# Recurrences with forget, input and candidate gates as three products, and attention's inputs in strips

## What is computed

```python
def rnn(x, h0, Wx, Wh, b):                       # layer 0
    h = tanh(x[t] @ Wx + b + h @ Wh)             # for t in 0..511
def lstm(x, h0, Wx, Wh, b):                      # layer 1
    a = x[t] @ Wx + b + h @ Wh                   # for t in 0..511
    i, f, o = sigmoid(a[:H]), sigmoid(a[H:2H]), sigmoid(a[2H:3H])
    g = tanh(a[3H:])
    c = f * c + i * g
    h = o * tanh(c)
x = x + rnn(x, cond, ...)
x = x + lstm(x, cond, ...)
x = x + transformer_block(x, cond, ...)          # layer 2: attention and feed-forward
x = x + mixture_of_experts(x, cond, ...)         # layer 3: two of four experts and a shared one
```

## Time and profile before

| | us |
|---|---|
| median of 3 runs | 2344.58 |
| lowest and highest | 2342.88, 2344.84 |
| the profiled execution | 2343.05 |
| its span | 2341.3 |
| recurrences: first and last write of `Hs` | 18.9, 1184.2 |
| PE, DVE, ACT, POOL busy | 2207.2, 1581.1, 1257.8, 560.5 |

### The profile page before, as it was taken

One profiled execution on the slowest core, in us unless ns is written; L12 is line 12 of the kernel. 1 busy time (PEld: TensorE's weight loads), 2 busy tenths in 40 slices (PEclk: granted clock), 3 DMA queues, 4 the chain that ended last, 5 costly groups with the idle time before them and its releaser, 6 DMA issues. The chain is left out here.

```text
span 2341.3 us, 94850 instructions
## 1 busy us (share of the span) xinstructions
PE 2207.2 (94%) x39004; PEld 1452.3 (62%) x39004; DVE 1581.1 (68%) x7316; ACT 1257.8 (54%) x4381; POOL 560.5 (24%) x1178
## 2 busy tenths in 40 slices
PE   8899999999999999999987699999999999999999
PEld 6677777777777777777743256464646556464666
DVE  5777777777777777777747684765747576674530
ACT  4555555555555555555565664647575564656432
POOL 0222222242221422214223031322213131221100
PEclk9999999999999999999998899999999999999999
DMA  4111111101000000000010200303030120302020
GB/s 119 36 38 31 38 40 42 37 25 32 29 31 27 22 27 29 31 27 18 23 69 1 88 35 1 131 1 131 1 131 1 38 94 1 131 1 104 0 86 9
DMA packets 51874, 102.64 MB, mean 44 GB/s; under 512 B 10468, under 2 KB 33380, under 8 KB 47348
## 3 DMA queue, kind: packets, MB, share of 16 engines
q1 hardware_dynamic: 48036, 94.06, 11.8%
q10 hardware_dynamic: 3408, 2.52, 0.4%
HBM read 75.53 MB, written 21.04 MB: 41 GB/s over the span
## 5 line engine op out<-in xcount | busy, mean ns | idle before, releaser
L135 PE MATMUL psFI<-wh,Hs 128*8 128x128 f32 (+3 forms) x8192 | 324.7, 276 | 61.0 <-DVE Hs L250 47.8
L135 PE MATMUL psOR<-wh,RH 128*16 128x128 f32 (+3 forms) x8320 | 321.5, 272 | 2.2 <-ACT RH L338 2.0
L135 PEld LDWEIGHTS psFI<-wh,Hs 128*8 128x8 f32 (+3 forms) x8192 | 182.2, 99 | 179.3 <-DVE Hs L250 179.3
L2054 ACT ACTIVATE pexp<-bank 128x1024 f32<-128x1024 f32 x256 | 244.3, 1023 | 36.1 <-PE bank L1384 35.9
L338 ACT ACTIVATE RH<-RT 128x16 f32<-128x16 f32 x512 | 110.9, 217 | 261.5 <-DVE RT L254 261.5
L1262 PE MATMUL bank<-x3T,ew 128*128 128x512 f32 x512 | 238.7, 593 | 0.0
L234 DVE STREAM_TRANSPOSE FIT<-psFI 128x128 f32<-128x128 f32 x512 | 162.0, 316 | 101.0 <-PE psFI L135 98.4
L329 ACT ACTIVATE sFI<-FIT 128x32 f32<-128x32 f32 x512 | 118.6, 232 | 200.4 <-DVE FIT L234 195.5
L135 PE MATMUL psG<-wh,Hs 128*8 128x64 f32 (+3 forms) x8192 | 208.6, 219 | 0.4 <-issue 0.4
L135 PEld LDWEIGHTS psOR<-wh,RH 128*16 128x16 f32 (+1 forms) x8320 | 205.7, 104 | 4.8 <-ACT RH L338 3.7
L1276 PE MATMUL bank<-ew,hidden 128*128 128x256 f32 x864 | 201.0, 379 | 0.0
(11 more groups left out here) (366 smaller groups left out, 4227.9 us busy)
## 6 DMA issues: line engine op xcount, KB each, us to landing
ew<-in_ew SPq DMA_DIRECT2D x32, 1024.0 KB, 9.1
qkv_scratch<-qkvr SPq DMA_DIRECT2D x31, 384.0 KB, 2.8
big<-qkv_scratch SPq DMA_DIRECT2D x7, 1536.0 KB, 7.8
XX<-in_xT SPq DMA_DIRECT2D x31, 256.0 KB, 2.7
x_scratch<-xr SPq DMA_DIRECT2D x32, 128.5 KB, 2.4
x<-x_scratch SPq DMA_DIRECT2D x8, 514.0 KB, 9.7
ada<-ada_scratch SPq DMA_DIRECT2D x8, 512.0 KB, 8.5
out_x<-x SPq DMA_DIRECT2D x7, 512.0 KB, 3.3
```

What stands on the lines that cost most here:

```text
L135: last = pe.matmul(bank[32 * j:32 * j + width, :], state(k), weights[:, k, j, cols], start=False, stop=k == KC - 1, tile_position=(0, 32 * ...
L2054: up(act.activation(M.pexp[:, n % 2, 2 * pr:2 * pr + 2, :], M.PS[pr][:, :, :], ACT.Exp, scale=1.0 / math.sqrt(HD)), "exps")
```

## The change

**Three products.** `psFI` becomes `psF` and `psI`, with 64 columns and two banks each. `FIT` becomes `FT` and `IT`. The loop makes the forget product, the input product and the candidate product, each with a raise of its semaphore (`FI` is raised twice a step). VectorE makes three transposes, ScalarE one sigmoid for forget and one for input. `gw` waits for forget's sigmoid only, the scan for input's too. The seeding bias copy and the inputs' product of the pair are split in the same way.

**Banks.** Both buffers of `psG` lie in one bank, and `psA` and `psB` share one. So TensorE waits at s = 2 for the next group's bias before it writes the candidate product, and for this slot's `GT` before it writes the inputs of the next group. The transposes of x2 wait until the outputs of q, k and v of the chunk two before have been taken (`qkv_out` instead of `zT_out`), also in `last_rows_back`.

**ScalarE's order.** The bias copies for s = 0, 1, 2, attention's copies and the heads' work stand ahead of the RNN's tanh (`tR`), not behind it; the bias copy at s = 3 stays behind.

**Strips.** Attention's 128 x 128 transposes and products in the loop go as four matmuls of 32 output partitions each, with a tile position for each (`strips`); the transposes become matmuls with the identity. VectorE still takes q, k and v out of `psB`.

```diff
@@ tensor, one slot
-                    products(R.psFI[g % 2], h, width, R.wh, F_I).then_inc(sem["FI"], 1)
+                    products(R.psF[g % 2], h, width, R.wh, F_).then_inc(sem["FI"], 1)
+                    products(R.psI[g % 2], h, width, R.wh, I_).then_inc(sem["FI"], 1)
+                    if s == 2 and g + 1 - FIRST < PIECES:
+                        pe.wait_ge(sem["bG"], g + 2 - FIRST)
                     products(R.psG[g % 2], h, width, R.wh, G_).then_inc(sem["G"], 1)
...
                 elif s == 1:
-                    inputs_of_group(g + 1, R.psFI, F_I, "bFI")
+                    inputs_of_group(g + 1, R.psF, F_, lambda q: (sem["bFI"], 2 * q + 1))
+                    inputs_of_group(g + 1, R.psI, I_, lambda q: (sem["bFI"], 2 * q + 2))
                 elif s == 2:
-                    inputs_of_group(g + 1, R.psG, G_, "bG", "X1")
+                    if lstm(i):
+                        pe.wait_ge(sem["gT"], n + 1)
+                    inputs_of_group(g + 1, R.psG, G_, lambda q: (sem["bG"], q + 1))
@@ vector, one slot
-                    dve.wait_ge(sem["FI"], n + 1)
-                    dve.transpose(flat(R.FIT), R.psFI[g % 2]).then_inc(sem["fiT"], 1)
+                    dve.wait_ge(sem["FI"], 2 * n + 1)
+                    dve.transpose(flat(R.FT), R.psF[g % 2]).then_inc(sem["fiT"], 1)
+                    dve.wait_ge(sem["FI"], 2 * n + 2)
+                    dve.transpose(flat(R.IT), R.psI[g % 2]).then_inc(sem["fiT"], 1)
                     dve.wait_ge(sem["G"], n + 1)
                     dve.transpose(flat(R.GT), R.psG[g % 2]).then_inc(sem["gT"], 1)
-                    dve.wait_ge(sem["sFI"], n + 1)
+                    dve.wait_ge(sem["sFI"], 2 * n + 1)
...
                     dve.wait_ge(sem["w"], n + 1)
+                    dve.wait_ge(sem["sFI"], 2 * n + 2)
                     dve.wait_ge(sem["tG"], n + 1)
@@ scalar, one slot
-                    act.activation(R.sFI[:, :, :, 1].rearrange("p g (k b) -> p (g k) b", k=KC), R.FIT[:, :, at_four:at_four + NB], ACT.Sigmoid).then_inc(sem["sFI"], 1)
+                    act.activation(by_block(second_scan(R.sFI[:, 0])), R.FT[:, :, at_four:at_four + NB], ACT.Sigmoid).then_inc(sem["sFI"], 1)
+                    act.wait_ge(sem["fiT"], 2 * n + 2)
+                    act.activation(by_block(second_scan(R.sFI[:, 1])), R.IT[:, :, at_four:at_four + NB], ACT.Sigmoid).then_inc(sem["sFI"], 1)
@@ attention's inputs
+        def strips(out, stationary, moving, start, stop):
+            for j in range(4):
+                at = slice(32 * j, 32 * j + 32)
+                last = pe.matmul(out[at], stationary[:, at], moving, start=start, stop=stop, tile_position=(0, 32 * j), skip_group_check=True)
+            return last
...
-                    last = pe.matmul(self.psB[:, half * P:(half + 1) * P], self.zT[:, k, :], self.wqkv[:, k, n * D + half * P:n * D + (half + 1) * P],
-                                     start=k == 0, stop=k == KC - 1, skip_group_check=True)
+                    last = strips(self.psB[:, half * P:(half + 1) * P], self.zT[:, k, :], self.wqkv[:, k, n * D + half * P:n * D + (half + 1) * P],
+                                  k == 0, k == KC - 1)
@@ last_rows_back
-        pe.wait_ge(*self.at("zT_out", c - 2))
+        pe.wait_ge(*self.at("qkv_out", c - 2))
```

More of the change, by code:

```diff
@@ L80 @@
     SLOTS = T + LAG
[L81 removed]
+    SIGNALS = ("FI", "G", "OR", "XX", "sFI", "tG", "sO", "tR", "tC", "bFI", "bG", "bOR", "fiT", "gT", "rT", "w", "c",
                "oT", "hL", "hR", "x1", "xx", "x2", "x_in_0", "x_in_1", "x_in_2", "ld_wx0", "ld_wh0", "ld_bias", "ld_states",
@@ L98, in __init__ @@
         self.zero = sb("zero", [P, P])
-        self.FIT, self.GT, self.RT = sb("FIT", [P, 2 * KC, 32]), sb("GT", [P, KC, 32]), sb("RT", [P, KC, 32])
+        self.FT, self.IT, self.GT, self.RT = (sb(n, [P, KC, 32]) for n in ("FT", "IT", "GT", "RT"))
         self.sFI, self.gw, self.cc = sb("sFI", [P, 2, KC * NB, 2]), sb("gw", [P, KC * NB, 2]), sb("cc", [P, KC * NB, 2])
@@ L102, in __init__ @@
         self.tC = sb("tC", [P, KC, NB])
-        self.psFI, self.psOR = ([ps(f"{n}{i}", 128) for i in range(2)] for n in ("psFI", "psOR"))
-        self.psG = [ps(f"psG{i}", 64) for i in range(2)]
+        self.psF, self.psI = ([ps(f"{n}{i}", 64) for i in range(2)] for n in ("psF", "psI"))
+        self.bothG = ps("psG", 128)
+        self.psG = [self.bothG[:, 64 * i:64 * i + 64] for i in range(2)]
+        self.psOR = [ps(f"psOR{i}", 128) for i in range(2)]
         self.sem = {n: ctx.enter_context(nc.semaphore(n)) for n in self.SIGNALS}
@@ L167, in inputs_of_group @@
                 x = piece_of(R.x1, q)
-                last = products(bank[g % 2], lambda k: x[:, k, :], 32, R.wx, cols)
-                if raises:
-                    last.then_inc(sem[raises], 1)
+                products(bank[g % 2], lambda k: x[:, k, :], 32, R.wx, cols)
             inputs_made = F.tensor_engine(pe, lambda c: R.x2[c % 2], sem["x2"])
             pe.wait_ge(sem["zeroed"], 1)
-            for bank in R.psOR + R.psFI + R.psG:
+            for bank in R.psOR + R.psF + R.psI + [R.bothG]:
                 last = pe.matmul(bank, R.zero[:, :], R.zero[:, 0:bank.shape[1]], start=True, stop=True)
@@ L344, in _ @@
                     bias_of_pair(2 * g + 2)
-                else:
+                inputs_made(i)
+                Q.scalar_slot(act, i)
+                if rnn(i):
+                    act.wait_ge(sem["rT"], i + 1)
+                    act.activation(r_of(i), R.RT[:, :, at_pair:at_pair + NB], ACT.Tanh).then_inc(sem["tR"], 1)
+                if s == 3:
                     if lstm(i):
@@ L756, in slot @@
                         if c == 0:
-                            pe.wait_ge(self.ada_made, 2)
+                            pe.wait_ge(self.ada_made, 3)
                         if c >= 2:
-                            pe.wait_ge(*self.at("zT_out", c - 2))
+                            pe.wait_ge(*self.at("qkv_out", c - 2))
                     columns = self.psA[:, 0:D].rearrange("p (j k u) -> p j k u", k=KC, u=32)[:, :, o, :]
-                    last = pe.transpose(columns, x2(c)[:, o, :], self.W.I[:, :])
+                    last = strips(columns, x2(c)[:, o, :], self.W.I[:, :], True, True)
                     if o == 1:
@@ L768, in slot @@
                         pe.wait_ge(*self.at("xT_out", c + 1))
-                    last = pe.transpose(self.psA[:, k * P:(k + 1) * P], self.z[:, k * P:(k + 1) * P], self.W.I[:, :])
+                    last = strips(self.psA[:, k * P:(k + 1) * P], self.z[:, k * P:(k + 1) * P], self.W.I[:, :], True, True)
                     if k == 1:
@@ L806, in vector_engine @@
         C = self.vector
-        m, d, k, small, e, s1 = (self.S[:, i:i + 1] for i in (1, 5, 6, 9, 10, 13))
+        m, d, k, small, e = (self.S[:, i:i + 1] for i in (1, 5, 6, 9, 10))
         def slot(i):
@@ L1117, in kept_busy @@
         for _ in range(n):
-            pe.matmul(self.F.psA[:, :], self.F.wqkv[:, 0, 0:P], self.F.wqkv[:, 1, 0:512], start=True, stop=True)
+            pe.matmul(self.F.ps[:, :], self.F.wqkv[:, 0, 0:P], self.F.wqkv[:, 1, 0:512], start=True, stop=True)
     def last_transposes(self, pe):
```

33 lines of the change are left out of this document (13 added, 20 removed).

## The result

The changed kernel takes **2605.07 us** (median of 4 runs, 2600.39 to 2606.4) against 2344.71 for the kernel before on the same chip: 1.111 times as long, interval 1.109 to 1.113. The forecast was 2319.

A forecast was written before the change was run, and what follows sets the result against it. The recurrence's chain, 2.28 us a step, was taken as the bound. Gains of 15.8, 8.3 and 2.0 (26.1 us) off 2343.05, plus 0.4 tail, gave 2317.4, adjusted to the runs' median: 2319; range 2313 to 2326 (0.62).

The forecast's parts named there:

- What bounds the kernel: Recurrence loop: one chain of 2.28 us a step bounds it, not TensorE, which idles 0.25 us awaiting `Hs`.
- The three thin products: Gate products at each step's start: at 0.23 us each, the candidate product starts only 0.01 us later.
- (a): Gate products: candidate product comes later than 0.01 us; at +0.03, 2329 to 2333 us; chance 0.13.
- (b): Gate products: thin products go at their weight loads' pace, 0.27 or 0.34 us; 10 or 82 us slower; chance 0.07.
- The transposes: VectorE's gate transposes: 64-column ones take 0.23 to 0.24 us; `GT` about 0.95 after the first product in light steps.
- Rival (c): VectorE's gate transposes do not overlap, 0.23 us each; 2346 us, no change; chance 0.07.
- Some 0.07 us to spare: Candidate branch before the scan: slack beside the forget/input branch, contributing to a gain of 0.06 us a step.
- The strips: Attention's 128-wide products: four strips should save most of the 0.21 us idle issue, off the path; priced zero.
- The rival I gave to TensorE as the bound: Attention strips: were TensorE the bound, 14 products in each of 31 chunks save 91 us, giving 2252; chance 0.01.
- ScalarE's order: Bias copies ahead of the RNN's tanh: they fit into ScalarE's 0.49 us of idle time; price zero.
- The tail: First transpose behind the loop waits for the last `qkvr` and starts 0.4 us later: +0.4 us.
- Rival (d): TensorE's clock: the lighter engine falls to 1.2 GHz, some 0.6 us a step; far above 2400; chance 0.02.

The follow-up runs named there:

- light_order_b: light_b with the scan's three waits reordered so the tanh's is written first and the multiply's last: 2349.74 us (1.0026 of the kernel before).
- before_act: The kernel before with only ScalarE's new order (bias copies, attention's copies, heads' work ahead of the RNN's tanh): 2343.12 us (0.9993).
- after_two: The changed kernel with the scan's wait for input's sigmoid moved to the multiply, leaving the scan two waits: 2614.83 us (1.115).
- pad13: The kernel before with 13 tiny matmuls of zeros and their loads added per step in steps 40 to 499: 2590.38 us (1.106).
- pad7: The kernel before with 7 tiny matmuls of zeros and their loads added per step: 2417.56 us (1.032).
- nostrips: The changed kernel with attention's transposes and products 128 wide again, one instruction in place of four: 2548.40 us (1.088).
- before_strips: The kernel before with only attention's transposes and products split into strips: 2348.01 us (1.0019).
- thin_light: The changed kernel without strips and without the inputs' products of forget, input and candidate gate in steps 40 to 500: 2494.42 us (1.064).
- light_b: The changed kernel without strips, every inputs' product of steps 40 to 499 cut to a single matmul: 2385.56 us (1.018).
- before_swap_b: The kernel before with the scan's two waits swapped, the tanh's ahead of the multiply's: 2377.47 us (1.0147).

## Where the prediction was right and where it failed

**What bounds the kernel.** Right for the kernel before: the chain of one step. Wrong as a statement about what can bound it. I read the busy time of TensorE and its clock and took "waits 0.25 us a step" for room. The room in instructions, 58.7 against some 66 per us, was 12%, and the change asked for 40% more. No step of the working counted them: their price was put at nothing without a reason, and this is the step that cost most, some 242 us. Counting what `products` and the strips write, 132 loads and matmuls a step against 184, would have been the first sign.

**The three thin products.** They start at 419.93, 420.17 and 420.39: the candidate product 0.46 behind the first, as forecast. Rivals (a) and (b), a slower pace of the products, did not come. What a thin product costs is not its place in the row but 32 more instructions a step, 16 loads and 16 matmuls, and the inputs' product of it.

**The transposes.** `FT` comes 0.49 behind the first product, `IT` 0.22 later, `GT` 0.22 after that, at 0.93 (forecast about 0.95, light steps). They take 0.25 rather than 0.23. Rival (c) is refuted: `IT` and `GT` start when their products allow.

**"Some 0.07 us to spare".** This is the step that failed in the critical path. The sum takes the scan to start 0.03 behind the tanh. With the tanh's wait last in a row of three it starts 0.13 behind, and 0.10 was already there in the earlier trace rows, which I read as slack of 0.07. From `GT` to the scan it is 0.63 in the step above, not 0.52 (and 0.59 before). Instead of -0.06 a step came out at +0.036: 511 x 0.036 = 18 us. light_order_b shows the -0.06 once the wait is placed so.

**The strips.** Their idle issue of 0.2 us did go; priced at zero, they cost 57 us in after (2605.07 - 2548.40) through 12 instructions a step. The rival I gave to TensorE as the bound looked at idle time per product, the wrong quantity, and it counts 14 such products a chunk where there are 16.

**ScalarE's order.** Price zero, right (before_act).

**The tail.** The first transpose behind the loop waits for the last `qkvr`, as said:

```profile
1445.71 0.48 DVE L871 SCALAR_TENSOR_TENSOR qkvr<-psAB,Sr,bqkv 128x256 f32<-128x256 f32 x1
...
1446.33 0.41 PE L588 MATMUL psAB<-I,x2c 128*128 128x128 f32 x2 [1.58 <-DVE qkvr L871]
```

1446.33 is 1.06 behind the last `Hs` (1445.27), against 0.58 in the earlier trace rows: +0.48, forecast +0.4.

**The clock.** Rival (d) did not come: 1.00 in the stretch above, 0.99 over the span.

**The account.** Of 260 us in the loop, 18 are the longer step; the other 242, by subtraction, are the supply of instructions. The direct count for 100 to 1100 us: 235 of 258 block boundaries with a gap of over 0.3 us, 210 us together. The 356 steps in it are longer than undisturbed ones by 356 x (2.805 - 2.305) = 178 us; the rest of the gaps, I take it, fell where TensorE would have waited for `Hs` anyway.

What sets 3.8 us for a block stays open. In after its parts are, as medians, 1.26 us from the start of a block to the start of the next packet, 1.10 for the packet and 1.39 from its landing to the next block. Packets were never closer than 3.3 us in any of these kernels. No run here changed anything but the number and spacing of instructions.

## What to carry to other kernels

Count the instructions of each engine per step beside its busy time: splitting a wide fp32 product into thin ones, or a 128-wide one into strips, multiplies their number and hardly shows in busy time, and TensorE got at most some 66 per us here. Idle "issue" at changing products, at equal distances in instructions, is its sign. A gap of 0.1 us between a releaser's end and an instruction with several waits is not slack before it has been compared with a hand-over by a single wait; the semaphore that comes last belongs into the wait written first.

## What the runs showed of the hardware

Three things I had not expected. TensorE's instructions arrive in packets of 256, and in five kernels with 162 to 186 instructions a step (after, after_two, pad13, pad7, nostrips) packets came 3.85 to 3.93 us apart in the mean, whatever the instructions were (matmuls of zeros in pad13, gates in after): 65 to 66.4 per us. At 64 per us only 4 us were lost (before_strips). How much the supply keeps in reserve is not settled: thin_light, with a mean rate of 59 per us, waited 0.79 us behind its dense blocks, while in light_b 13 single blocks that executed in 2.9 to 3.2 us among ones of 4.4 were followed by 0.05. And the order in which two waits are written moved this kernel by 34 us (before_swap_b), and the order of three by 36 (light_order_b), 0.07 to 0.08 us in a step.
